# A graph network on one core: the tiles of a linear attention moved closer together and earlier in the edge stage

## The chip, the cores and the metric
One core of a Trainium2 chip runs the whole program in one launch. The metric is device time in microseconds. The kernel before took 3404.61 us, the median of three runs (3399.55 to 3411.63). TensorE multiplies matrices, VectorE and ScalarE do elementwise work, GpSimd issues the indirect gathers and scatters here, SyncE (SP) issues plain transfers and passes on semaphores; ScalarE issues some plain transfers as well.

## The reference
There are 12500 nodes with 256 features and 200000 edges, sorted by target. The targets are drawn as 12500 times the square of a uniform number, so nodes with small numbers have far more edges. Cut to what matters:

```
xn  = layernorm(x)
# graph attention, 4 heads, with a self loop at each node
h   = xn @ W;  e = leaky_relu(a_src[src] + a_dst[dst]);  alpha = softmax of e over each target's edges
gnn = relu(layernorm(segment_sum(h[src] * alpha, dst) + bias + xn))
# linear attention over all nodes, 8 heads
q, k, v = rmsnorm(xn) @ w_qkv;  q, k = elu(q) + 1, elu(k) + 1
kv  = sum over nodes of k (x) v;   z = 1 / (q . sum k)
hm  = xn + (q . kv * z) @ w_out + b_out;   mix = hm + rmsnorm(hm)
x   = x + gnn + mix
x   = x + mixture of 8 experts, top 2 (layernorm(x))
```

## The kernel before, in words
The program has stages with a barrier between them: a projection of all nodes (to about 200 us), the edge stage `attend_edges` (205 to 2266 us) and a last stage with the experts.

The edge stage works on 391 blocks of 512 sorted edges and 98 windows of 128 target nodes. A block that crosses from one window to the next is worked on once for each, so there are 391 + 98 - 1 = 488 *pairs* of a block and a window. At the start, where a window has thousands of edges, nearly every pair brings a new block; at the end three pairs share about two blocks. For each block GpSimd issues four gathers (L1147), which bring the rows of the edges' source nodes into a ring of 6 blocks. For each pair VectorE makes one-hot rows of the targets (L1203); TensorE transposes them (L1405) and multiplies out the targets' scores (L1415); VectorE and ScalarE make the weights (L1209 to L1221, L1312 to L1319); VectorE weighs the gathered rows (L1227); TensorE sums them by target (L1425), three pairs later in its order; VectorE adds the sum to the window (L1244).

A gather waits for a free slot of its ring. SP tells of one in `track`: it waits until the rows of a block have come (L1109) and until an earlier block's pairs are all weighed (L1116), and counts up the semaphore on which GpSimd waits.

Between the pairs lie the tiles of the linear attention, 98 tiles of 128 nodes, each twice. The *first tile* (K/V): ScalarE loads the turned rows (`load_rT`, L1325); TensorE multiplies out K, V and Q (L1437, L1440) into PSUM tiles that have one copy; ScalarE takes Relus and exponentials (`exponents`, L1332 to L1341); VectorE makes keys and queries (`elu`, L1252 and L1253); ScalarE stores the queries (`store_q`, L1345); TensorE adds keys times values to a sum (`accumulate`, L1449). The *second tile* (mixing) needs that sum complete: attend (L1459), divide, turn (L1468), project out (L1482), add and store.

Nothing is scheduled by a machine. Each engine's program is the same loop over pairs, written out by `in_pairs`, and two tables, `KV_AT` and `MIX_AT`, say at which pair a tile stands. Each step has a number of pairs by which it is late or early to that:

```
SP   track(q): wait msg_ready of the block before; count up slot_free; fetch the next targets
ACT  (KV_AT, -3, load_rT), (KV_AT, 0, exponents), (KV_AT, 3, store_q)
PE   (KV_AT, 3, accumulate), (KV_AT, 0, kv_and_q)
DVE  (KV_AT, 3, elu)
load_rT(t):    wait kv_psum >= t - 1      # the product of tile t-2, whose buffer it takes
exponents(t):  wait kv_psum >= t + 1
elu(t):        wait q_stored of tile t-2  # the store of the buffer it writes
kv_and_q(t):   wait keys, q and v of tile t-1
```

Steps of one table that fall into the same pair stand in the order of these lists. `elu` of a tile comes in VectorE's order behind the weighing (L1227) of the pair at which the tile stands.

Of the kernel before, what the change touches and what calls it, by code (L numbers as in the profile page):

```python
# [16 lines left out]
TILES = (N + P - 1) // P  # L17
# [18 lines left out]
PAIRS = SUPERS + WINDOWS - 1  # L36
# [904 lines left out]


KV_FIRST = 4
KV_END = KV_FIRST + 7 * TILES // 3
MIX_FIRST = KV_END + 14
LAST_PAIR = PAIRS - 12
AHEAD = 1.15


def paced():  # L950
    at = {}
    for t in range(TILES):
        part = (AHEAD - math.sqrt(AHEAD * AHEAD - 4 * (AHEAD - 1) * t / TILES)) / (2 * (AHEAD - 1))
        at[MIX_FIRST + int((LAST_PAIR - MIX_FIRST) * part)] = t
    return at


KV_AT = {KV_FIRST + 7 * t // 3: t for t in range(TILES)}
MIX_AT = paced()
assert len(MIX_AT) == TILES  # L960
assert len(MIX_AT) == TILES


def attend_edges(nc, s, plan, x, w_out, b_out, out):


    with ExitStack() as ctx:
# [113 lines left out]
        def in_pairs(steps, lag, at=()):  # L1081
            for n in range(PAIRS + max(lag)):
                for k, step in enumerate(steps):
                    if 0 <= n - lag[k] < PAIRS:
                        step(n - lag[k], (n - lag[k]) % PAIR_RING)
                for table, late, step in at:
                    if n - late in table:
                        step(table[n - late])

        with nc.Block() as block:  # L1090
# [68 lines left out]
            def _(v):  # L1159
# [135 lines left out]
                def measure(t):  # L1295
# [3 lines left out]
                in_pairs([own_row, one_hot, fold, add_sum, score, leaky, weigh, look_up], [0, 1, 2, 6, 2, 2, 3, 0],  # L1299
                         [(KV_AT, 3, elu), (KV_AT, 6, keep_kv), (MIX_AT, 2, divide), (MIX_AT, 5, add_xn), (MIX_AT, 5, measure)])  # L1300

            @block.scalar
            def _(act):
# [74 lines left out]
                def store_hh(t):  # L1378
# [8 lines left out]
                in_pairs([bound, copy_hot, weights], [1, 0, 1],  # L1387
                         [(KV_AT, -3, load_rT), (KV_AT, 0, exponents), (KV_AT, 3, store_q),
                          (MIX_AT, -3, load_mix), (MIX_AT, 0, normalise), (MIX_AT, 2, store_xn), (MIX_AT, 3, copy_headsT),
                          (MIX_AT, 6, store_hh)])  # L1390
                act.wait_ge(blank_stored, 16)
# [5 lines left out]
            def _(pe):  # L1397
# [73 lines left out]
                def project_out(t):  # L1471
# [9 lines left out]
                    for c in range(C):  # L1481
# [6 lines left out]
                in_pairs([turn_hot, target_scores, sum_pair], [0, 0, 3],  # L1488
                         [(KV_AT, 3, accumulate), (KV_AT, 0, kv_and_q),
                          (MIX_AT, 4, project_out), (MIX_AT, 2, turn_heads), (MIX_AT, 0, attend)])  # L1490

# [1092 lines left out]
```

## Time and profile before

| | |
|---|---|
| median of three runs | 3404.61 us |
| the profiled execution | 3406.47 us, span 3404.8 us |
| TensorE busy | 2790.3 us (82%) |
| VectorE busy | 2314.5 us (68%) |
| GpSimd busy | 2147.9 us (63%) |
| ScalarE busy | 1294.8 us (38%) |
| edge stage | 205 to 2266 us |

The busy shares are means over stages with different limits; a stretch of the edge stage has to be read by itself. A gather is busy for 953 ns and the next follows after a pause that the profile calls "issue", so GpSimd at its full pace still shows a quarter of its time idle.

### The profile page before, as it was taken

Reading aid. Unit: us, or ns where it says so; the run is one execution under the profiler, and the core shown is the slowest. Engines: PE = TensorE matmul, PEld = TensorE weight load, DVE = VectorE, ACT = ScalarE, POOL = GpSimd, SP = SyncE. Lnnn points to the kernel's source line nnn. Section 1 sums busy time; section 2 is a strip of 40 time slices with the busy share of each in tenths; the row PEclk is TensorE's granted clock in tenths of the full one; section 3 lists DMA queues with packets and bytes.
Section 4 is the critical chain, followed back from the end, with each engine's and each line's share of the span. In section 5 each row is a group of like instructions: output and inputs, shape, how many; then the busy total and the mean of one; then the engine's idle time right before and its main releaser. Section 6 shows DMA issues by size and latency. Waiting matters only on the chain. (4 is left out here: it accounts for less than half of the span.)

```text
span 3404.8 us, 69111 instructions
## 1 busy us (share of the span) xinstructions
PE 2790.3 (82%) x17326; PEld 2267.9 (67%) x17327; DVE 2314.5 (68%) x6562; ACT 1294.8 (38%) x4267; POOL 2147.9 (63%) x2115
## 2 busy tenths in 40 slices
PE   5857888888889887888888888865396888989997
PEld 4635656666666665666666666654386878889997
DVE  6655666666666666777777777788887887655553
ACT  5713333333333333333333333335464555423332
POOL 3167777777777777666666666634475766654443
PEclk9969999999999999999999999985597999999999
DMA  7645666666666656666665666646676778754443
GB/s 258 251 121 156 160 157 158 159 160 163 162 163 162 163 150 182 182 181 182 176 180 166 177 175 169 166 129 204 216 198 187 212 195 236 179 113 71 72 71 50
DMA packets 409375, 562.80 MB, mean 165 GB/s; under 512 B 66164, under 2 KB 339271, under 8 KB 408890
## 3 DMA queue, kind: packets, MB, share of 16 engines
q0 software_dynamic: 114496, 265.49, 33.1%
q1 hardware_dynamic: 209784, 216.35, 21.5%
q10 hardware_dynamic: 84770, 77.19, 7.1%
q8 instruction: 134, 2.20, 0.3%
q14 instruction: 191, 1.56, 0.2%
HBM read 427.31 MB, written 132.72 MB: 164 GB/s over the span
## 5 line engine op out<-in xcount | busy, mean ns | idle before, releaser
L1147 POOL DMA_INDIRECT rows<-node_rows,index x1552 | 1479.4, 953 | 567.3 <-issue 452.6
L1425 PE MATMUL ps_sum<-msg,hot 128*128 128x260 f32 x3904 | 1021.2, 407 | 19.8 <-DVE big L1244 3.7
L1425 PEld LDWEIGHTS ps_sum<-msg,hot 128*128 128x128 f32 x3904 | 731.6, 197 | 137.0 <-issue 8.5
L1227 DVE TENSOR_TENSOR msg<-rows,ps_w 128x1024 f32<-128x1024 f32 x488 | 596.2, 1222 | 35.8 <-ACT ps_w L1319 20.2
L1958 POOL DMA_INDIRECT out_dram<-big x204 | 364.7, 1788 | 338.8 <-DVE big L2224 186.0
L2098 PE MATMUL x_ps_hT<-wq,x_w_ring 128*128 128x128 f32 x3264 | 412.6, 281 | 50.4 <-DVE x_w_ring L2191 29.0
L2098 PEld LDWEIGHTS x_ps_hT<-wq,x_w_ring 128*128 128x128 f32 x3264 | 406.3, 197 | 70.5 <-DVE x_w_ring L2191 35.0
L1203 DVE TENSOR_SCALAR hotT<-targets,pair_node_id 128x512 bf16 x488 | 186.6, 382 | 356.2 <-SPq L1109 354.0
L2018 ACT ACTIVATE wq<-x_ps_hT,x_b1T 128x128 f32<-128x128 f32 x816 | 233.4, 369 | 509.4 <-PE x_ps_hT L2098 504.6
L1405 PE MATMUL ps_hot<-ident_h,hotT 128*128 128x128 bf16 x1952 | 195.0, 223 | 264.9 <-DVE hotT L1203 262.0
L1405 PEld LDWEIGHTS ps_hot<-ident_h,hotT 128*128 128x128 bf16 x1952 | 128.1, 99 | 363.6 <-DVE hotT L1203 351.5
L1312 ACT ACTIVATE e<-e 128x16 f32<-128x16 f32 x488 | 106.2, 218 | 667.1 <-DVE e L1221 652.8
L1947 POOL DMA_INDIRECT expert_in<-f_rows,f_slot x196 | 239.0, 1220 | 180.2 <-DVE f_rows L2359 90.5
L1307 ACT ACTIVATE hot<-ps_hot 128x512 f32<-128x512 bf16 x488 | 286.9, 588 | 43.2 <-PE ps_hot L1405 42.2
L2118 PE MATMUL x_ps_out<-x_w_ring,wq 128*128 128x256 f32 x864 | 211.4, 389 | 0.0
L1244 DVE TENSOR_TENSOR big<-big,ps_sum 128x260 f32 x488 | 202.4, 415 | 8.6 <-issue 5.4
L1437 PE MATMUL ps_kv<-wq,area 128*128 128x512 f32 x392 | 191.4, 611 | 10.1 <-DVE area L1253 9.3
L1293 DVE TENSOR_TENSOR area<-ps_kv,area 128x256 f32<-128x256 f32 x98 | 41.6, 425 | 210.2 <-PE ps_kv L1482 210.2
L2182 DVE COPY wq<-x_ps_t 128x256 f32<-128x256 f32 x204 | 86.0, 421 | 141.3 <-PE x_ps_t L2083 137.5
L2118 PE MATMUL x_ps_out<-big,wq 128*128 x768 | 181.5, 379 | 0.0
L1332 ACT ACTIVATE area<-ps_kv 128x256 f32<-128x256 f32 x98 | 37.7, 385 | 366.0 <-PE ps_q L1440 359.1
L2118 PEld LDWEIGHTS x_ps_out<-x_w_ring,wq 128*128 128x128 f32 x864 | 161.3, 197 | 18.4
(310 smaller groups left out, 4297.6 us busy)
## 6 DMA issues: line engine op xcount, KB each, us to landing
targets<-dst_row SPq DMA_DIRECT2D x391, 128.0 KB
x_w_ring<-in_L_ffn_W_dram SPq DMA_DIRECT2D x62, 512.0 KB, 5.2
big<-expert_in SPq DMA_DIRECT2D x204, 130.0 KB, 2.1
rows<-node_rows,index POOLq DMA_INDIRECT x1564
node_rows<-big SPq DMA_DIRECT2D x14, 924.0 KB
turned<-rT SPq DMA_DIRECT2D x14, 896.0 KB, 4.6
area<-turned ACTq DMA_DIRECT2D x98, 128.0 KB
queries<-area ACTq DMA_DIRECT2D x98, 128.0 KB
```

Of the source, the lines that this page charges most:

```text
L1147: g.indirect_dma_start(rows[:, j, k, :], None, s.node_rows, bass.IndirectOffsetOnAxis(ap=index[:, b, j * G + k:j * G + k + 1], axis=0)).th ...
L1227: v.tensor_tensor(m[:, :, 0:D].rearrange("p g (h f) -> p g h f", h=GH), rows[:, bass.ds(here, 1), :, 0:D].rearrange("p j g (h f) -> p (j g ...
L1244: v.tensor_tensor(dest, dest, ps_sum[:, j % 2, 0:SUM], ALU.add).then_inc(sum_added, 1)
L1307: act.activation(hot[:, j % MSGS, :], ps_hot[:, 0:SPAN], ACT.Copy).then_inc(hot_ready, 1)
L1405: mm = pe.transpose(ps_hot[:, k * P:(k + 1) * P], hotT[:, j % 2, k * P:(k + 1) * P], ident_h[:, :])
L1425: mm = pe.matmul(ps_sum[:, j % 2, 0:SUM], hot[:, j % MSGS, k * P:(k + 1) * P], msg[:, j % MSGS, k, :], start=(k == 0), stop=(k == G - 1))
L1437: pe.matmul(ps_kv[:, :], rT[:, u, c * P:(c + 1) * P], s.wq[:, c, D:3 * D], start=(c == 0), stop=(c == C - 1))
L1947: g.indirect_dma_start(s.expert_in, bass.IndirectOffsetOnAxis(ap=slot[0:count, j, k, i:i + 1], axis=0), rows[0:count, j, i, :], None).then ...
L1958: g.indirect_dma_start(out, bass.IndirectOffsetOnAxis(ap=x_rows[:, j, D:D + 1].bitcast(I32), axis=0), outs[:, j, :], None, compute_op=ALU. ...
L2018: ins = act.activation(actT[:, j % 2, c, :], ps_hT[:, j % 2, c * P:(c + 1) * P], ACT.Gelu, bias=b1T[:, bass.ds(e * HC + c, 1)])
L2098: mm = pe.matmul(ps_hT[:, j % 2, k * P:(k + 1) * P], w_ring[:, u, a:a + P], x_rowsT[:, j % 2, c, :], start=(c == 0), stop=(c == C - 1))
L2118: mm = pe.matmul(ps_out[:, j % 2, 0:D], actT[:, j % 2, c, :], w, start=(c == 0), stop=(c == HC - 1))
```

## The change
Only the two tables change. Before, a first tile stood every 7/3 pairs, from pair 4 to 230, and the second tiles from pair 246 to 473, 2 or 3 pairs apart and getting wider. Now a first tile stands every 3/2 pairs (4, 5, 7, 8, 10, 11, ... 149), and the second tiles stand every 9/4 pairs from pair 165 to 383 (gaps of 2, 2, 2, 3). The last 104 pairs have no tile. No instruction is added or taken away.

```
-KV_END = KV_FIRST + 7 * TILES // 3
+KV_END = KV_FIRST + 3 * TILES // 2
 MIX_FIRST = KV_END + 14
-KV_AT = {KV_FIRST + 7 * t // 3: t for t in range(TILES)}
-MIX_AT = paced()
+KV_AT = {KV_FIRST + 3 * t // 2: t for t in range(TILES)}
+MIX_AT = {MIX_FIRST + 9 * t // 4: t for t in range(TILES)}
```

What this does to the order shows on two engines. First ScalarE among the first tiles. In the kernel before (`area<-turned` is the load of a tile's turned rows, L1332 to L1341 the Relus, the copy of V and the exponentials of another tile, `queries<-area` a store; L1312 to L1319 belong to the pairs):

```order
L1325 DMA area<-turned 128x256 [waits k_kv_psum]
L1312 ACTIVATE e<-e 128x16 [waits c_e_ready]
L1307 ACTIVATE hot<-ps_hot 128x512 [waits c_sum_psum,c_turned]
L1317 ACTIVATE msg<-e 128x4x4 [waits c_sum_psum,c_e_bounded]
L1319 ACTIVATE ps_w<-e 128x16 [waits c_msg_ready]
L1332 ACTIVATE area<-ps_kv 128x256 [waits k_q_ready,k_kv_psum]
L1333 ACTIVATE area<-ps_q 128x256
L1337 ACTIVATE values<-ps_kv 128x2x128 [waits k_acc_done,k_ones_set]
L1341 ACTIVATE area<-area 128x512 [waits k_bounded]
L1345 DMA queries<-area 128x256 [waits k_q_ready]
```

And of the changed kernel, whose lines are numbered 9 lower (L1316 is the load, L1323 to L1332 the tile's work, L1336 the store):

```order
L1303 ACTIVATE e<-e 128x16 [waits c_e_ready]
L1298 ACTIVATE hot<-ps_hot 128x512 [waits c_sum_psum,c_turned]
L1308 ACTIVATE msg<-e 128x4x4 [waits c_sum_psum,c_e_bounded]
L1310 ACTIVATE ps_w<-e 128x16 [waits c_msg_ready]
L1316 DMA area<-turned 128x256 [waits k_kv_psum]
L1323 ACTIVATE area<-ps_kv 128x256 [waits k_q_ready,k_kv_psum]
L1324 ACTIVATE area<-ps_q 128x256
L1328 ACTIVATE values<-ps_kv 128x2x128 [waits k_acc_done,k_ones_set]
L1332 ACTIVATE area<-area 128x512 [waits k_bounded]
L1336 DMA queries<-area 128x256 [waits k_q_ready]
```

The load and the store, which stood in different pairs, now stand in the same pair around each tile's work. The load has moved from the pair before to right ahead of the first Relu: it is that of the tile two later and waits for the product that the Relu reads. The store is that of the tile two before.

Then TensorE in the same place. Before, from one K/V product (`ps_kv<-wq,area` and `ps_q<-area,wq`) to the next, with two pairs between:

```order
L1437 MATMUL ps_kv<-wq,area 128x512 x2
L1440 MATMUL ps_q<-area,wq 128x128 x4
L1405 MATMUL ps_hot<-ident_h,hotT 128x128 x4
L1410 TENSOR_LOAD pair_window
L1415 ISA
L1415 MATMUL ps_tgt<-reach_parts,hotT 128x24 x4
L1425 MATMUL ps_sum<-msg,hot 128x260 x4
L1405 MATMUL ps_hot<-ident_h,hotT 128x128 x4
L1415 ISA
L1415 MATMUL ps_tgt<-reach_parts,hotT 128x24 x4
L1425 MATMUL ps_sum<-msg,hot 128x260 x4
L1437 MATMUL ps_kv<-wq,area 128x512 x2
```

And at one of the short gaps of the changed kernel:

```order
L1428 MATMUL ps_kv<-wq,area 128x512 x2
L1431 MATMUL ps_q<-area,wq 128x128 x4
L1396 MATMUL ps_hot<-ident_h,hotT 128x128 x4
L1406 ISA
L1406 MATMUL ps_tgt<-reach_parts,hotT 128x24 x4
L1416 MATMUL ps_sum<-msg,hot 128x260 x4
L1440 MATMUL ps_acc<-values,area 128x129 x2
L1428 MATMUL ps_kv<-wq,area 128x512 x2
L1431 MATMUL ps_q<-area,wq 128x128 x4
```

Every second tile now has one pair to the next one instead of two or three, and each product has an accumulation right ahead of it.

## Rows read from the trace of the kernel before

**Rows 1.** Timeline, GpSimd, the last block: start us, us, engine, line, operation
```profile
2246.24 0.95 POOL L1147 DMA_INDIRECT rows<-node_rows,index  x1 [0.30 <-issue]
...
2250.00 0.97 POOL L1147 DMA_INDIRECT rows<-node_rows,index  x1 [0.30 <-issue]
```

**Rows 2.** Stretches: length, busy us (x) PE PEld DVE ACT POOL, clock, DMA, GB/s
```profile
222.00:889.00 667.00, 559.09 (x3294) 416.01 (x3293) 415.44 (x1080) 222.94 (x824) 505.59 (x530) 0.97 0.62 159
889.00:959.00 70.00, 59.79 (x368) 44.66 (x367) 42.73 (x110) 24.95 (x92) 53.05 (x56) 1.00 0.61 162
959.00:1863.00 904.00, 770.57 (x4768) 579.47 (x4769) 629.16 (x1695) 310.42 (x1115) 646.90 (x681) 0.98 0.64 172
1863.00:2266.00 403.00, 346.61 (x2168) 266.50 (x2166) 303.01 (x817) 133.17 (x493) 260.27 (x274) 0.96 0.59 162
```

**Rows 3.** First and last stretch, VectorE's one-hot rows alone (L1203, one a pair)
```profile
222.00:889.00 667.00, 56.23 (x144) 0.97 0.62 159
...
1863.00:2266.00 403.00, 39.05 (x104) 0.96 0.59 162
```

**Rows 4.** Groups by line, the gathers, 222 to 1235 us and 1288 to 2215 us
```profile
L1147 POOL DMA_INDIRECT rows<-node_rows,index x806 | 768.5, 953 | 245.7 <-issue 234.1 <-SPq L1116 11.6
...
L1147 POOL DMA_INDIRECT rows<-node_rows,index x666 | 634.3, 952 | 294.8 <-issue 194.4 <-SPq L1116 100.4
```

**Rows 5.** Timeline, one first tile and the next, all engines
```profile
962.21 1.88 PE L1437 MATMUL ps_kv<-wq,area 128*128 128x512 f32 x4
...
965.02 0.38 ACT L1332 ACTIVATE area<-ps_kv 128x256 f32<-128x256 f32 x1 [3.44 <-PE ps_q L1440]
...
965.72 0.33 ACTq L1345 DMA_DIRECT2D queries<-area  x1
...
967.04 0.21 ACT L1319 ACTIVATE ps_w<-e 128x16 f32<-128x16 f32 x1
...
968.52 0.42 DVE L1252 SCALAR_TENSOR_TENSOR area<-ps_kv,area 128x256 f32<-128x256 f32 x1
...
969.52 1.96 PE L1437 MATMUL ps_kv<-wq,area 128*128 128x512 f32 x4
```

**Rows 6.** Timeline, TensorE, a tile with two pairs and an accumulation
```profile
1201.67 1.88 PE L1437 MATMUL ps_kv<-wq,area 128*128 128x512 f32 x4
...
1204.28 0.39 PE L1405 MATMUL ps_hot<-ident_h,hotT 128*128 128x128 bf16 x4
...
1206.44 0.61 PE L1449 MATMUL ps_acc<-values,area 128*128 128x129 f32 x4
...
1209.05 1.88 PE L1437 MATMUL ps_kv<-wq,area 128*128 128x512 f32 x4
```

**Rows 7.** Timeline, ScalarE's issue of a load of turned rows
```profile
1005.24 0.35 ACTq L1325 DMA_DIRECT2D area<-turned  x1
```

**Rows 8.** Transfers: what, queue, count, size of one, median us to landing
```profile
turned<-rT SPq DMA_DIRECT2D x14, 896.0 KB, 4.6
...
expert_in<-f_blank SPq DMA_DIRECT2D x9, 130.0 KB, 3.0
...
out_dram<-c_blank ACTq DMA_DIRECT2D x1, 128.0 KB, 1.7
```

**Rows 9.** Timeline, TensorE's attend at pairs 289 and 298, 313 and 322
```profile
1477.47 0.50 PE L1459 MATMUL ps_acc<-kv,area 128*128 128x132 f32 x3
...
1513.90 0.50 PE L1459 MATMUL ps_acc<-kv,area 128*128 128x132 f32 x3
...
1576.36 0.50 PE L1459 MATMUL ps_acc<-kv,area 128*128 128x132 f32 x3
...
1613.42 0.62 PE L1459 MATMUL ps_acc<-kv,area 128*128 128x132 f32 x4
```

**Rows 10.** Stretches, as rows 2: pairs without tiles, and one of a later stage
```profile
1235.00:1286.00 51.00, 36.01 (x202) 27.27 (x202) 32.24 (x90) 11.92 (x48) 38.51 (x42) 0.87 0.58 145
2300.00:2400.00 100.00, 52.46 (x241) 50.10 (x242) 89.57 (x222) 48.64 (x104) 42.57 (x33) 0.50 0.65 219
```

More of the change, by code:

```diff
@@ L943 @@
 KV_FIRST = 4
-KV_END = KV_FIRST + 7 * TILES // 3
+KV_END = KV_FIRST + 3 * TILES // 2
 MIX_FIRST = KV_END + 14
[L946 to L955, printed above, removed]
-KV_AT = {KV_FIRST + 7 * t // 3: t for t in range(TILES)}
-MIX_AT = paced()
+KV_AT = {KV_FIRST + 3 * t // 2: t for t in range(TILES)}
+MIX_AT = {MIX_FIRST + 9 * t // 4: t for t in range(TILES)}
+assert len(KV_AT) == TILES and max(MIX_AT) + 8 < PAIRS
 assert len(MIX_AT) == TILES
```

## The prediction
> **What bounds the kernel now.** I read the table of stretches first, with the edge stage (205 to 2266 us) cut where the new schedule will change what it does, then the gather line's idle time, then single rows. GpSimd issues four gathers for each block of 512 edges, and a gather starts every (2250.00 - 2246.24) / 3 = 1.253 us when nothing holds it [rows 1]: 5.01 us per block. The four stretches of the edge stage hold 530, 56, 681 and 274 gathers in 667, 70, 904 and 403 us [rows 2], the first of them 144 pairs and the last 104 [rows 3]. At 1.253 us the gathers alone take 664, 70, 853 and 343 us. So the first two stretches run at the pace of the gathers; the last two, where the second tiles lie now, lose 51 and 60 us. The gather line says the same: until 1235 us it waited 11.6 us for a free slot of the ring (released by SP's track, L1116), from 1288 to 2215 us 100.4 us [rows 4]. In the second half the engines bind, in the first half the gathers. There are 391 blocks whatever the schedule, so the question is only how long GpSimd stands still.
>
> **First tiles, 1.5 pairs apart: +114 us.** 98 K/V tiles, which lay in the first 228 pairs, now start in 145 (pairs 4 to 149): 97 periods. At 667 us a period would be 6.9 us. The rows of one undisturbed tile show what it needs [rows 5]. TensorE starts K/V at 962.21; ScalarE's first Relu follows at 965.02 (2.81 later); the pair's weights are out at 967.04 plus 0.21; VectorE, which must weigh that pair first, reads the tile from 968.52; and TensorE may write K/V again at 969.52. The PSUM tile has one copy, so 7.31 us is the least period of the chain, whatever the spacing. TensorE's own work would fit: a tile with two pairs and an accumulation takes 1209.05 - 1201.67 = 7.38 us, a pair 1206.44 - 1204.28 = 2.16 [rows 6].
>
> The chain gets longer in two ways, and both are seen in ScalarE's order. The load of a later tile, which stood an iteration apart from the Relus, now stands right ahead of them and waits for the same K/V product. Its issue takes 0.35 us [rows 7], in which ScalarE can't issue the Relu: 7.31 + 0.34 = 7.65. And the store of the tile two before, whose buffer VectorE overwrites, is issued only behind this tile's exponentials: 965.72 - 965.02 = 0.70 us after the first Relu [rows 5], so 2.81 + 0.34 + 0.70 = 3.85 after K/V starts, while VectorE would begin at 968.52 - 962.21 + 0.34 = 6.65. It has 2.80 us to land. The trace shows no landing for this store. The nearest rows are 1.7 us (128 KB on ScalarE's queue, alone) and 3.0 us (130 KB, several together); 4.6 us for seven times the bytes is the far end [rows 8]. So the period is prolonged by 0 to 1.8 us; nearest to the 3.0 row it is 0.2. I add another 0.2 because the store now goes out 1.0 us behind a 128 KB load on the same queue: an estimate. Period 7.31 + 0.34 + 0.40 = 8.05 us, 97 x 8.05 = 781 us, against 667: +114. The bounds are 97 x 7.38 = 716 (neither the issue nor the store adds anything) and 97 x 9.45 = 917 (the store takes 4.6). Behind the load's issue queue ScalarE's Relus, and behind them the next pair's weights; behind VectorE's late read queue the next pair's one-hot and so TensorE's transposes. That is the chain itself, and it is what the period counts. TensorE has room in it: at a short gap its work is 7.38 - 2.16 = 5.22 us of 8.05. So has VectorE, busy for 415 us in this stretch [rows 2]. Nothing hides the period itself: once the ring of gathered rows is full, SP frees a slot only when a block has been weighed, and GpSimd stands.
>
> The Trainium skill (DMA: Bandwidth & Descriptors, Anatomy of one DMA) gives a DMA about 2.0 us fixed plus its bytes over 436 GB/s, stated for the GpSimd path; for 128 KB that is an estimate of 2.3 us, under the 2.80. By it the store would cost nothing; the rows of this size, 1.7 and 3.0, lie on both sides of it.
>
> **The 16 pairs between: -12 us.** Before, 56 gathers took 70 us here. After an engine-bound part the ring is ahead: a gather may run until six blocks are held, of which about 3.5 are in work or under way, so some 2.4 blocks x 5.01 = 12 us are there already (an estimate). TensorE needs 16 x 2.16 = 35 us, so the gathers, 70 - 12 = 58 us, still set it.
>
> **Second tiles, every 2, 2, 2 and 3 pairs: 0.** The old table has the same pattern in places. From one attend to the fourth after it, nine pairs on, it is 1513.90 - 1477.47 = 36.43 and 1613.42 - 1576.36 = 37.06 us [rows 9], mean 36.75. The 97 gaps are 24.25 such groups: 891 us. The gathers of these pairs take 853 in all, but at the front, where a block makes only 1.25 pairs, nine pairs are 7.2 blocks, 36 us: hardly less than the engines' 36.75, so some jitter of both is added. I put 891 + 13 = 904 us, as before, with 880 to 930 as bounds. The tiles' own wait, VectorE on TensorE's output projection, is the one they have now.
>
> **The last 104 pairs without tiles: -45 us.** Gathers 343 us, and 15 us from the last gather's end (2250.97) to the stage's end [rows 1], is 358 against 403. TensorE needs 104 x 2.16 = 225, and is covered. What comes after the edge stage is unchanged.
>
> **Sum.** +114 - 12 + 0 - 45 = +57 us. The profiled execution took 3406.47 us (span 3404.8); that is 1.9 over the median of the three timed ones, 3404.61. So 3406.5 + 57 - 1.9 = 3461.6; I say 3460. In plain terms, the 100 us that GpSimd waits late are halved, and more than 110 us of new waiting come early, where there was none.
>
> **Rivals.**
> - *The first part is still covered by the gathers* (faster). If consecutive K/V tiles overlapped, or the chain shortened, the part would stay at 667 and the ring never fill: 0 + 0 + 0 - 45, 3360 us. It decides if the period falls under 6.9. For it speaks that TensorE is 84% busy there now (559.09 of 667 [rows 2]) and DVE less; against it, that no K/V starts before the tile's second reader is done, so that 7.31 stands.
> - *The store lands in its slack and at most the load's issue counts* (about no change). Period 7.38 to 7.65: 716 to 742, the sum -8 to +18, 3397 to 3423 us. For it: the 1.7 us row. Against: the 3.0 row and the load in front.
> - *The store is as late as 4.6 us*: +136 on the forecast, 3596. For it: the DMA engines are 0.62 busy in this stretch as it is [rows 2]. Against: the store is a seventh of the 4.6 row's bytes.
> - *The tail runs cold.* The granted clock fell to 0.87 in the tile-free stretch 1235 to 1286 us, and to 0.50, the lower of the two levels (1.2 GHz), in a later stage [rows 10]. If the whole tail ran at the lower one, a pair would take 4.32 instead of 2.16, over the gathers' 343 / 104 = 3.30: 104 x 1.02 = +106, 3566 us. Against it: in that very stretch 42 gathers took 51 us, 1.21 each, the full pace.
>
> The Trainium skill (TensorE: Matmul & The Clock Gate, Loop structure matters more than you think) has it that waiting for a DMA between matmuls lets the clock drop. By that rule the tail would be this last rival; the trace agrees that the clock dips there, with 0.87, and not that time is lost.
>
> **How the numbers follow.** Forecast (period 7.75 to 8.5, 3431 to 3505 us) 0.60; store in its slack 0.18; first part covered 0.08; late store 0.07; cold tail 0.07. About 0.3%, 10 us, is what a measurement can tell here. Faster: 0.08 and a little of the slack case, 0.10. Same: most of the lower half of the slack case and an edge of the forecast's, 0.14. Slower: the rest, 0.76. The range leaves out the covered case below and most of the late store and the cold tail above: 3400 to 3525.
>
> **What would show it.** K/V starts 8.05 us apart on average at both gaps, with pair 149 near 1003 us instead of 889; GpSimd's wait for slots over 80 us before pair 149 and under 60 in all the second tiles; VectorE idle ahead of its first K/V read behind the store; the last 104 pairs in about 358 us with gathers 1.25 apart. I am wrong if the periods are under 7.4 us, if the last pairs lose the gathers' pace, or if the second tiles' nine pairs come out far from 37 us.

## The result, and the profile after
The changed kernel takes 3536.02 us (median of six runs, 3528.68 to 3555.2), the kernel before 3401.32 in the same session: a ratio of 1.0399 [1.0369, 1.0429], 135 us slower. The forecast was 3460, with a range to 3525. The direction was right, the size too small.

The trace of after is of the slowest of its six runs, 19 us over the median (span 3553.5). It is 149 us longer than the trace of before. By the start of VectorE's one-hot of a pair (one a pair, as in [rows 3]), the edge stage divides like this:

| stretch | before, us | after, us | difference | forecast |
|---|---|---|---|---|
| pairs 4 to 149, first tiles | 670.8 | 862.6 | +191.8 | +114 |
| pairs 149 to 165, no tiles | 70.5 | 63.1 | -7.4 | -12 |
| pairs 165 to 384, second tiles | 904.4 | 911.4 | +7.0 | 0 |
| pair 384 to the end of the stage | 402.9 | 356.1 | -46.8 | -45 |
| all after the stage | 1138.6 | 1139.9 | +1.3 | 0 |

Only the first line is far off. The table of stretches of after has the same cuts, moved to where these pairs now lie. Columns as in [rows 2]: length, busy us (instructions) of PE, PEld, DVE, ACT, POOL, then the granted clock, DMA share, GB/s.

```profile
225.00:1083.00 858.00, 694.20 (x3831) 509.05 (x3831) 445.52 (x1145) 262.32 (x960) 515.76 (x538) 0.92 0.51 136
1083.00:1146.00 63.00, 48.68 (x300) 37.63 (x298) 42.43 (x116) 18.46 (x73) 43.73 (x46) 0.95 0.52 140
1146.00:2057.00 911.00, 764.27 (x4751) 574.40 (x4752) 655.16 (x1797) 304.37 (x1067) 647.16 (x683) 0.98 0.67 182
2057.00:2413.00 356.00, 283.05 (x1717) 217.70 (x1715) 252.00 (x641) 106.11 (x425) 258.70 (x273) 0.92 0.53 133
```

Beside [rows 2] the first line is the one to read. It holds nearly the same gathers as before (538 in place of 530), but over 858 us and not 667. Every engine is idle for longer, DMA falls from 0.62 to 0.51, and the clock falls from 0.97 to 0.92. The idle time is one of waiting for one another. The table of waits of that stretch names the links (engine, line, what it waited for: us in all, times, longest us). L1107 is SP's track, L1116 before; L1428 is the K/V product, L1437 before.

```profile
POOL rows L1138 <- SPq L1107: 197.0, 84, 8.5
PE ps_kv L1428 <- DVE area L1244: 139.9, 49, 3.9
DVE area L1243 <- DMA queries<-area: 23.0, 47, 1.5
PE ps_hot L1396 <- ACT hot L1298: 20.2, 44, 0.8
```

GpSimd now waits 197.0 us for slots of the ring where until 1235 us it waited 11.6 in [rows 4]; so the gathers no longer set the pace. TensorE waits 139.9 us, in 49 places, for VectorE to be done with the K/V tile. In the kernel before that same wait is a small row (the table of waits of before, 222 to 889 us):

```profile
PE ps_kv L1437 <- DVE area L1253: 7.6, 22, 0.4
```

The last stretch of after is as it was forecast: the last 104 pairs run at the gathers' pace, at a clock of 0.92, where it was 0.96. GpSimd's timeline (start us, us, engine, line, operation) has its gathers 1.24 and 1.26 us apart:

```profile
2390.27 0.94 POOL L1138 DMA_INDIRECT rows<-node_rows,index  x1 [0.30 <-issue]
2391.51 0.95 POOL L1138 DMA_INDIRECT rows<-node_rows,index  x1 [0.30 <-issue]
2392.77 0.95 POOL L1138 DMA_INDIRECT rows<-node_rows,index  x1 [0.30 <-issue]
```

**Where the first part's time goes.** The first and the last K/V product of the part, on TensorE's timeline:

```profile
225.13 1.06 PE L1428 MATMUL ps_kv<-wq,area 128*128 128x512 f32 x1
...
1091.33 0.67 PE L1428 MATMUL ps_kv<-wq,area 128*128 128x512 f32 x1 [1.93 <-DVE area L1244]
```

That is (1091.33 - 225.13) / 97 = 8.93 us a period, where 8.05 was forecast. The two kinds of gap differ. On average a period with one pair in it (short) takes 8.30 us, one with two (long) 9.59; the last short one is left out of the means here, since no load stands ahead of its Relu. One of each, all engines, from the timeline (in square brackets the idle time before, and what ended it):

```profile
700.04 0.33 ACTq L1316 DMA_DIRECT2D area<-turned  x1
700.47 0.38 ACT L1323 ACTIVATE area<-ps_kv 128x256 f32<-128x256 f32 x1 [4.34 <-PE ps_q L1431]
701.17 0.33 ACTq L1336 DMA_DIRECT2D queries<-area  x1
...
704.28 0.42 DVE L1243 SCALAR_TENSOR_TENSOR area<-ps_kv,area 128x256 f32<-128x256 f32 x1 [0.22 <-DMA queries<-area]
...
705.28 3.40 PE L1428 MATMUL ps_kv<-wq,area 128*128 128x512 f32 x4 [2.67 <-DVE area L1244]
...
709.61 0.33 ACTq L1316 DMA_DIRECT2D area<-turned  x1
710.04 0.38 ACT L1323 ACTIVATE area<-ps_kv 128x256 f32<-128x256 f32 x1 [7.34 <-PE ps_q L1431]
...
711.47 0.61 ACT L1298 ACTIVATE hot<-ps_hot 128x512 f32<-128x512 bf16 x1
712.22 0.38 PE L1396 MATMUL ps_hot<-ident_h,hotT 128*128 128x128 bf16 x4 [0.48 <-ACT hot L1298]
...
713.87 0.41 DVE L1244 SCALAR_TENSOR_TENSOR area<-ps_q,area 128x256 f32<-128x256 f32 x1
...
714.50 0.61 PE L1440 MATMUL ps_acc<-values,area 128*128 128x129 f32 x4
...
714.94 1.88 PE L1428 MATMUL ps_kv<-wq,area 128*128 128x512 f32 x4
```

The chain is the one of [rows 5]: product, Relu, VectorE's read, next product. The load (L1316) is issued between the product and the Relu, and VectorE's read waits for the store (`queries<-area`), as was forecast. The table of transfers of after also has what the trace of before lacked, that store's median time to landing, here of the stores at the short gaps:

```profile
queries<-area ACTq DMA_DIRECT2D x98, 128.0 KB, 3.2
```

That is the 2.80 us of slack and the 0.40 of delay that the forecast gave it. What the forecast has not is the product that starts at 705.28. It comes after a stall of 2.67 us and takes 3.40 us, where the next, at 714.94, takes 1.88 and those of [rows 5] 1.88 and 1.96. The table of stretches has the clock around it: the stall, the slow product, and the next product that isn't slow.

```profile
702.60:705.28 2.68, 0.02 (x1) 0.03 (x1) 2.22 (x4) 0.10 (x2) 2.07 (x3) 0.91 0.57 162
705.28:708.70 3.42, 3.42 (x6) 1.63 (x7) 0.35 (x2) 0.00 (x0) 1.06 (x2) 0.57 0.31 90
714.94:718.00 3.06, 3.06 (x23) 2.09 (x22) 2.62 (x7) 0.00 (x0) 2.45 (x3) 1.00 0.47 122
```

The granted clock is 0.57 in the slow product, so most of it ran at the lower level (1.2 GHz), and 1.00 in the next. TensorE is stalled ahead of all 48 products that open a long gap, 139.9 / 49 = 2.9 us on average, but only some are slow: the product with the queries' takes 4.23 us or more in 31 of them, and 2.85 in the other 17. One of the 17, behind a stall of 2.95 us (TensorE's timeline, then the stretch of the product, clock 1.00):

```profile
672.30 1.96 PE L1428 MATMUL ps_kv<-wq,area 128*128 128x512 f32 x4 [2.95 <-DVE area L1244]
```

```profile
672.30:675.15 2.85, 2.85 (x15) 1.88 (x16) 0.35 (x2) 0.00 (x0) 2.16 (x3) 1.00 0.61 157
```

So a stall of this length doesn't lower the clock each time; what decides it, no run here shows. The 4.08 us below are the mean of both kinds.

The mean of each link of the chain, over all gaps of a kind, with what the forecast had for it:

| link, us | forecast | short | long |
|---|---|---|---|
| K/V and query product | 2.81 | 2.79 | 4.08 |
| its end to the Relu (issue of the load) | 0.34 | 0.47 | 0.47 |
| Relu to VectorE's first read (exponentials, store) | 3.90 | 4.02 | 3.59 |
| both reads, to the next product | 1.00 | 1.02 | 1.45 |
| period | 8.05 | 8.30 | 9.59 |

The short gap is 0.25 over the forecast, the long one 1.54, of which 1.27 is the product at the lower clock. The store costs 0.31 less there than was forecast, and the last link 0.45 more: VectorE has read the tile at 714.28 (713.87 + 0.41), but TensorE comes from the second pair, whose transposes waited for ScalarE's copy until 712.22, and has an accumulation ahead of the product. Times their number: 48 x 0.25 + 48 x 1.54 = 86 us, less 0.7 for the last short gap: the 97 x (8.93 - 8.05) = 85 that the first part lacks. These means are of the slowest run. The same first part in the first experiment below, in its fastest run, has 8.27 and 9.33 us, so the mean of the long gaps is known to some 0.3 us.

### The profile page after: what moved, and what is told of

Same layout as the page of the kernel before. It is cut to its first block and busy times, and to the rows that moved or that the text cites. A ratio compares the mean times of both kernels' runs of the same rounds, so it can differ in the third digit from the quotient of the medians.

```text
span 3553.5 us, 69111 instructions
## 1 busy us (share of the span) xinstructions
PE 2845.9 (80%) x17326; PEld 2301.8 (65%) x17327; DVE 2319.0 (65%) x6562; ACT 1294.8 (36%) x4267; POOL 2150.6 (61%) x2115
## 5 line engine op out<-in xcount | busy, mean ns | idle before, releaser
L1428 PE MATMUL ps_kv<-wq,area 128*128 128x512 f32 x392 | 235.7, 733 | 141.9 <-DVE area L1244 141.9
L1200 DVE TENSOR_REDUCE e<-ps_tgt 128x32 f32<-128x96 f32 x488 | 121.6, 249 | 226.8 <-PE ps_tgt L1406 223.9
L1323 ACT ACTIVATE area<-ps_kv 128x256 f32<-128x256 f32 x98 | 37.6, 384 | 579.7 <-PE ps_q L1431 579.7
L1428 PEld LDWEIGHTS ps_kv<-wq,area 128*128 128x128 f32 x392 | 79.7, 225 | 212.1 <-issue 211.9
```

The source lines that it names most:

```text
L1428: pe.matmul(ps_kv[:, :], rT[:, u, c * P:(c + 1) * P], s.wq[:, c, D:3 * D], start=(c == 0), stop=(c == C - 1))
```

## The experiments
**Theory.** The first part is bound by the chain of one K/V tile. The chain is prolonged by the load's issue, by the store, and by the product that runs at the lower clock after TensorE's stall. **Rivals.** That the second tiles take part in the loss; that the load, or the store, explains most of it by itself; that the slow products only go along with the stall and cost nothing.

A ratio is to the kernel before, timed beside the experiment (medians of 3399.71 to 3407.5 us). "Less than the changed kernel" goes by its 3536.02 us from another session, so a few us mean nothing there.

**Each half alone.** Both edits are made to the kernel before.

```
-KV_AT = {KV_FIRST + 7 * t // 3: t for t in range(TILES)}
+KV_AT = {KV_FIRST + 3 * t // 2: t for t in range(TILES)}
```

> Only the first tiles are moved (1.5 pairs apart, pairs 4 to 149); the second tiles keep the pairs they had before (246 to 473). Theory (the whole loss is made in the first part: a K/V period of about 8.9 us instead of the 6.9 that the gathers give, 97 times): slower than before by some 185 us less the 12 of the refilled ring, about 3575 us; GpSimd's wait for slots about 200 us before pair 149. Rival (the second tiles, standing closer, cost the time): about as before, 3400 us.

Measured: 3583.38 us, 1.0538 [1.0509, 1.0567], near the 3575 expected. The dense first tiles alone are worse than the whole change, since the second tiles stay late.

```
-MIX_AT = paced()
+MIX_AT = {MIX_FIRST + 9 * t // 4: t for t in range(TILES)}
```

> Only the second tiles are moved, to every 9/4 pairs from pair 246 to 464; the first tiles stay 7/3 pairs apart. Theory: 24.25 groups of nine pairs at 36.75 us are 891 us where the old table took 919 for its 97 gaps, and the ten pairs freed at the end run at the gathers' pace: 0 to 25 us faster than before, about 3386 us. Rival (the second tiles cost the time): slower by about the 135 us of the whole change.

Measured: 3409.69 us against 3406.46, 1.0008 [0.9997, 1.0019]; the expected gain didn't come. From pair 246 to 464 it took 910 us (before 894), from there to pair 487 it took 67.5 (before 75). Denser second tiles cost about what the free pairs behind them bring, if they begin as late as before. So the loss is all in the first tiles. That the 47 us won in the tail come from the second tiles' earlier start follows by subtraction (3583 - 3536 = 47), since neither half alone has that start.

**The load and the store, one iteration elsewhere.** From here to all three repairs together the edits are made to the changed kernel.

```
-[(KV_AT, -3, load_rT), (KV_AT, 0, exponents), (KV_AT, 3, store_q),
+[(KV_AT, -2, load_rT), (KV_AT, 0, exponents), (KV_AT, 3, store_q),
```

> The changed kernel with the load of the turned rows one pair later in ScalarE's order (2 pairs ahead of its tile instead of 3), so that the product it waits for is an older one and its issue no longer stands between the K/V product and the first Relu. Theory: the first Relu follows the product's end by 0.04 us instead of 0.47, the period falls by 0.4 us, 97 times: 35 to 42 us faster than the changed kernel, about 3497 us. Rival (ScalarE's issue of a load costs nothing there): 3536 us, unchanged.

Measured: 3489.91 us, 1.0249 [1.0229, 1.0269], 46 less than the changed kernel. Its timeline has the Relu right behind the product, and the load's issue behind the tile's work:

```profile
650.39 1.05 PE L1431 MATMUL ps_q<-area,wq 128*128 128x128 f32 x8
651.48 0.38 ACT L1323 ACTIVATE area<-ps_kv 128x256 f32<-128x256 f32 x1 [3.91 <-PE ps_q L1431]
652.17 0.33 ACTq L1336 DMA_DIRECT2D queries<-area  x1
653.07 0.33 ACTq L1316 DMA_DIRECT2D area<-turned  x1
654.98 0.42 DVE L1243 SCALAR_TENSOR_TENSOR area<-ps_kv,area 128x256 f32<-128x256 f32 x1
655.98 2.85 PE L1428 MATMUL ps_kv<-wq,area 128*128 128x512 f32 x4 [1.93 <-DVE area L1244]
```

From the product's end (651.44) to the Relu it is 0.04 us, in place of 0.47. The store is still issued 0.69 us behind the Relu, so its slack is the same, but the load now follows it in the queue. VectorE's wait for it nearly goes, in the table of waits:

```profile
DVE area L1243 <- DMA queries<-area: 4.9, 9, 1.1
```

So the load cost more than its own issue, since it also stood ahead of the store. The short gaps are 7.55 us on average, the long ones 9.08, with the product still at 4.01.

```
-[(KV_AT, -3, load_rT), (KV_AT, 0, exponents), (KV_AT, 3, store_q),
+[(KV_AT, -3, load_rT), (KV_AT, 0, exponents), (KV_AT, 2, store_q),
```

> The changed kernel with the store of the queries one pair sooner (2 pairs after its tile instead of 3), so that at least one other tile's work lies between the store and the read that needs its buffer. Theory: at the short gaps VectorE's first K/V read follows the first Relu by 3.50 us instead of 4.02, at the long ones by 3.50 instead of 3.59: 49 x 0.52 + 48 x 0.09 = 30 us faster than the changed kernel, about 3506 us; more if TensorE's shorter stall keeps its clock up. Rival (the store lands in its slack): unchanged, 3536 us.

Measured: 3517.9 us, 1.0327 [1.0307, 1.0347], 18 less than the changed kernel. Here no row of VectorE waiting for the store is left in the first part. VectorE reads 661.57 - 658.07 = 3.50 us after the Relu at a short gap (mean 3.54, in place of 4.02):

```profile
658.07 0.38 ACT L1323 ACTIVATE area<-ps_kv 128x256 f32<-128x256 f32 x1 [4.33 <-PE ps_q L1431]
...
661.57 0.42 DVE L1243 SCALAR_TENSOR_TENSOR area<-ps_kv,area 128x256 f32<-128x256 f32 x1
```

That is the least that [rows 5] show, 968.52 - 965.02. The store costs 0.5 us at the short gaps and little at the long ones.

```
-[(KV_AT, -3, load_rT), (KV_AT, 0, exponents), (KV_AT, 3, store_q),
+[(KV_AT, -2, load_rT), (KV_AT, 0, exponents), (KV_AT, 2, store_q),
```

> The changed kernel with both the load one pair later and the store one pair sooner. Theory: short gaps 7.31 us, the bare chain; long gaps 9.1 us as with the later load alone, if the shorter stall still lets the clock fall, and 7.9 if not: 97 periods of 8.2 or 7.6 instead of 8.93, 70 to 130 us faster than the changed kernel, 3405 to 3466 us. Rival (the two repairs overlap, since the later load also frees the store's queue): no faster than the later load alone, 3490 us.

Measured: 3485.01 us, 1.0249 [1.0210, 1.0288], by the ratio no faster than with the load alone, as the rival had it: with the load later, only 4.9 us of the wait for the store were left to win. The short gaps come to 7.36, the bare chain of [rows 5]. The long ones stay at 9.10, with a product of 4.03, so the expectation was wrong that the clock would come back with a shorter stall. The table of waits from 225 to 1030 us, and the timeline with a slow product between two that aren't:

```profile
PE ps_kv L1428 <- DVE area L1244: 97.3, 49, 4.0
```

```profile
652.91 1.88 PE L1428 MATMUL ps_kv<-wq,area 128*128 128x512 f32 x4
660.23 2.44 PE L1428 MATMUL ps_kv<-wq,area 128*128 128x512 f32 x4 [1.93 <-DVE area L1244]
669.31 1.88 PE L1428 MATMUL ps_kv<-wq,area 128*128 128x512 f32 x4
```

The stall is 97.3 / 49 = 2.0 us now, and the clock still falls behind it in 35 of 48 places (0.93 over the part).

**Filling the stall.** Ten extra products for each two tiles, put ahead of the K/V product that is slow, keep TensorE at work while VectorE reads. They write into the bank in which the K/V sum is kept, so that sum is changed.

```
+FILL = 10
...
+if t % 2:
+    for k in range(FILL):
+        pe.matmul(ps_acc[:, 384:512], s.ident[:, :], s.wq[:, 0, 0:128], start=True, stop=True, ...)
```

> The changed kernel, where TensorE does ten more 128x128x128 f32 products (some 2.1 us at full clock; their result is not read) ahead of each K/V product at a short gap, in the 2.9 us in which it stands idle there. Theory (the stall of TensorE lets the granted clock fall, and the K/V product behind it, which takes 4.08 us on average instead of 2.79, runs partly at the lower level): the product is back at 2.8 us, the clock of the first part above 0.97 instead of 0.92, 48 x 1.25 = 60 us faster than the changed kernel, about 3476 us. Rival (that product is slow for another reason, its operands or the DMA): unchanged at 3536 us or slower by what sticks out of the fill.

Measured: 3498.06 us, 1.0289 [1.0251, 1.0327], 38 less than the changed kernel with 490 more products in the part. First its table of stretches, then its timeline:

```profile
225.00:1060.00 835.00, 764.58 (x4953) 604.12 (x4951) 462.29 (x1191) 270.87 (x993) 532.48 (x556) 1.00 0.53 144
```

```profile
705.85 2.40 PE L1425 MATMUL ps_acc<-wq,ident 128*128 128x128 f32 x20
...
709.79 1.95 PE L1432 MATMUL ps_kv<-wq,area 128*128 128x512 f32 x4 [1.55 <-DVE area L1245]
```

The clock is 1.00 over the whole part, the product 2.88 us with the queries', and the long gaps fall from 9.59 to 8.38. One product of the 48 is slow, the first. So it was the clock that made them long, and the clock fell because TensorE stood still. The gain is less than the 60 expected. The short gaps got 0.2 longer (8.50; VectorE's read comes later after the Relu, 4.24 on average in place of 4.02), and most of that is the store, by the table of waits (225 to 1060 us; 23.0 us in 47 places in the changed kernel):

```profile
DVE area L1244 <- DMA queries<-area: 30.6, 44, 2.0
```

Also, the 9.59 is of the slowest run of the changed kernel.

Now all three repairs together. The fill is seven products, added onto columns of that bank which nothing reads (and which one product more, ahead of the pairs, sets to begin with).

```
-[(KV_AT, -3, load_rT), (KV_AT, 0, exponents), (KV_AT, 3, store_q),
+[(KV_AT, -2, load_rT), (KV_AT, 0, exponents), (KV_AT, 2, store_q),
+FILL = 7
...
+if t % 2:
+    for k in range(FILL):
+        pe.matmul(ps_acc[:, 384:512], s.ident[:, :], s.wq[:, 0, 0:128], start=False, stop=False, ...)
```

> The changed kernel with all three repairs: the load one pair later, the store one pair sooner, and seven products of TensorE (some 1.5 us, added onto columns that are not read) in its stall at the short gaps. Theory (these three are all that the first part lost beyond the bare chain): short gaps 7.4 us, long ones 7.8, 97 periods of 7.6 instead of 8.93: 129 us faster than the changed kernel, 3407 us, about the kernel before, since the bare chain alone is still longer than the 6.9 us of the gathers. Rival (something else holds the first part too): 3440 us or more.

Measured: 3428.7 us against 3399.71, 1.0081 [1.0056, 1.0105]. The stretch, and GpSimd's wait for slots from 205 to 1000 us:

```profile
225.00:970.00 745.00, 719.01 (x4593) 561.90 (x4592) 450.38 (x1163) 268.86 (x981) 518.63 (x543) 1.00 0.60 158
```

```profile
POOL rows L1139 <- SPq L1108: 73.0, 55, 5.5
```

Clock 1.00, short gaps 7.36, long ones 7.92, and from the first K/V product to the last (962.75 - 221.97) / 97 = 7.64 us. Of the changed kernel's 135 us that takes away 107. No product of the 48 is slow. Beside the run with load and store moved, the fill is the only difference, and it brings 3485.01 us to 3428.7; 48 x (9.10 - 7.92) = 57. But the chain is still longer than the 6.9 us that the gathers of a period allow, so GpSimd still stands, and the kernel is still slower than before. None of these repairs brings the mean of the short gaps under 7.36, the chain through the one PSUM tile; a second copy of that tile was not tried.

**Another spacing.** At two pairs to a tile a period has 2 x 670.8 / 145 = 9.25 us of gathers, more than the chain needs. The first edit is made to the changed kernel, the next adds wider second tiles, and the third is made to the kernel before.

```
-KV_AT = {KV_FIRST + 3 * t // 2: t for t in range(TILES)}
+KV_AT = {KV_FIRST + 2 * t: t for t in range(TILES)}
```

> Other tables: a first tile every 2 pairs (4 to 198), the second tiles every 9/4 pairs from 214 to 432, 55 pairs without. Theory: two pairs bring 1.6 to 1.9 blocks, 8 to 9.6 us of gathers, more than the chain of 7.3 to 8 us, so the first part stays at the gathers' pace, TensorE has no long stall, and the load and store stand in pairs of their own; the second tiles lose 24.25 x 36.75 = 891 us against 807 of gathers, less 12 of the ring: 72 us of standing still in all against 102 before. About 34 us faster than before, 3367 us. Rival (any first part denser than 7/3 pairs is bound by the chain): slower than before.

Measured: 3391.57 us against 3407.5, 0.9963 [0.9943, 0.9983]: 16 us faster, half of what was expected. The first part is covered again: from 205 to 1100 us GpSimd waited 10.4 us for slots (206.5 in the changed kernel, 8.8 before). The rest waits 103.1 us, like before (105.9), where 72 in all were expected: the second tiles every 9/4 pairs cost as much as the old ones.

```
-MIX_AT = {MIX_FIRST + 9 * t // 4: t for t in range(TILES)}
+MIX_AT = {MIX_FIRST + 27 * t // 10: t for t in range(TILES)}
```

> Other tables: a first tile every 2 pairs (4 to 198), the second tiles every 2.7 pairs from 214 to 475, none in the last 12. Theory: 29 gaps of two pairs at 8.4 us and 68 of three at 10.7 are 972 us, against 957 of gathers in these pairs: GpSimd hardly stands still, 35 us in all with jitter instead of 102. About 68 us faster than before, 3335 us. Rival (a long tile-free end is what pays): slower than with the second tiles every 9/4 pairs.

Measured: 3358.6 us, 0.9885 [0.9845, 0.9925]: 49 us faster than before, where 68 were expected. With the second tiles spread over nearly all the pairs that are left, the late wait for slots falls to 52.9 us, not to the 35 expected.

```
-LAST_PAIR = PAIRS - 12
+LAST_PAIR = PAIRS - 9
-KV_AT = {KV_FIRST + 7 * t // 3: t for t in range(TILES)}
+KV_AT = {KV_FIRST + 2 * t: t for t in range(TILES)}
```

(with `KV_END` at `KV_FIRST + 2 * TILES`; the second tiles keep the old widening pace, from pair 214.)

> Other tables: a first tile every 2 pairs (4 to 198), the second tiles from pair 214 to 476 by the old pacing, closer at first (2.3 pairs) and wider at the end (3.1), as fewer and fewer blocks come to a pair. Theory: GpSimd's wait for slots after 1100 us falls from 53 us (evenly every 2.7 pairs) to some 35: 15 to 20 us faster than that kernel, 60 to 65 faster than before, 3340 us. Rival (the jitter of both sides costs that much whatever the pacing): as with every 2.7 pairs, 3358 us.

Measured: 3351.26 us against 3399.71, 0.985 [0.983, 0.987], the lowest median here. But it is 48 us under the kernel before beside it, as the evenly spread tables were 49 under theirs, and the intervals overlap: the rival, that the pacing doesn't matter, stands. GpSimd's wait for slots, 205 to 1100 and 1100 to 2300 us:

```profile
POOL rows L1147 <- SPq L1116: 8.8, 29, 0.3
...
POOL rows L1147 <- SPq L1116: 47.6, 67, 3.6
```

The first part costs no wait, as in the kernel before, and the second half loses 58 us less (105.9 before). That is the 54 by which its edge stage ends earlier (2212.4 in place of 2266.2). Moving the tiles forward does gain; the place where the first tiles stop being covered lies between 2 and 1.5 pairs a tile.

## Why the prediction was wrong
- *The gathers bind early, the engines late, and the first part tips over*: right. The wait for slots moved from 11.6 to 197.0 us in the first part, where over 80 were named. The rival in which the gathers still cover that part fell.
- *The bare chain of 7.31 us*: right. With load and store out of the way the short gaps are 7.36.
- *The load's issue, 0.34*: it is 0.43 (0.47 against 0.04), and it delayed the store as well. Without it the kernel is 46 us faster.
- *The store, 0.40*: right at the short gaps (0.52 on average; it lands after 3.2 us in the median, the forecast's 2.80 + 0.40), too much at the long ones (0.1: 3.59 against the least 3.50). VectorE's idle time behind it was named in advance, and it is there: 23.0 us in 47 places. Neither the store in its slack nor the 4.6 us store came true. By the estimate of 2.3 us from the Trainium skill's figures for the GpSimd path (DMA: Bandwidth & Descriptors, Anatomy of one DMA) the store would have landed in time; the measurement, 3.2 us, decides, and it didn't.
- *97 periods of 8.05 us, both gaps alike, 781 us*: **this step failed**. At the short gaps the sum held within 0.25 us. At the long ones it lacked 1.54, of which 1.27 is the product at TensorE's lower clock (the fill gives 1.21 back) and the rest mostly TensorE's own order of work: I took 2.81 us for the product from a row in which TensorE hadn't waited, and noted that TensorE "has room" at a short gap. That room, 8.05 - 5.22 = 2.8 us of standing still, is the very stall of 2.9 us after which the clock falls in 31 places of 48; the fill shows it. The total, 866 us, lies inside the bounds of 716 to 917, but their upper end came from another cause, and my range cut it off.
- *The cold tail*: the lowered clock was weighed in the wrong stretch. The tail ran at 0.92 and lost nothing, since TensorE has slack there. By the rule of the Trainium skill named in the prediction (TensorE: Matmul & The Clock Gate, Loop structure matters more than you think), a long wait for a DMA between matmuls lets the clock drop. In the first part the wait is for VectorE, which that rule does not name; there the clock fell all the same, to 0.57 in the product behind a stall of 2.67 us.
- *The 16 pairs, -12, the second tiles, 0, and the tail, -45*: -7.4, +7.0 and -46.8. No run shows the 2.4 blocks that the -12 was made of. The second tiles' nine pairs came out at 37.27 us in one place (TensorE's timeline, an attend and the fourth after it), where 36.75 was forecast:

```profile
1602.86 0.61 PE L1450 MATMUL ps_acc<-kv,area 128*128 128x132 f32 x4
...
1640.13 0.61 PE L1450 MATMUL ps_acc<-kv,area 128*128 128x132 f32 x4
```

  Their wait for slots is 66.7 us, where I had named under 60.

What stays open: why the clock falls behind 31 of the 48 stalls and not behind the others of the same length, and why the store comes later in the fill. The savings of the load and of the store overlap (46 and 18 us apart, 51 together), since both shorten the same wait for the store.

## What to carry to other kernels
When a schedule is made denser, compare the chain of one tile (its only buffer, from the first write to the next) with the time that the bound resource gives it; as long as the chain is shorter the step is free, and beyond that each us counts as often as there are tiles. Where a chain makes TensorE stand still again and again, work out the sum with its next product at either clock; here the lower one came in 31 of 48 places and cost 1.27 us a long gap. Before work is packed, look for the spacing at which the cover just holds, and spread what is left over all the rest.

## What I had not expected of the hardware
- A stall of TensorE of 2.0 to 2.9 us, once in two periods (16 to 18 us), was enough for the lower clock in the product behind it, in 31 to 35 of 48 places: 4.03 to 4.08 us on average in place of 2.8. In the pair of gaps shown, the next product, without a stall, was at 1.00 again.
- Useless products in the stall made the kernel faster: ten brought the clock of the part from 0.92 to 1.00, seven, with load and store moved, from 0.93 to 1.00.
- A 0.33 us DMA issue on ScalarE's queue delayed the Relu behind it by 0.43, and the 128 KB load that it started delayed the store issued 1.1 us behind it so that VectorE waited: 23.0 us in 47 places, against 4.9 in 9 with the load behind the store.
